# Edge layer of a two-layer graph network: four products of nil matrices ahead of each step's sums

## What is computed

```python
def _L1_gnn_ref(x, src, dst, W_w, W_b, U_w, U_b, V_w, V_b, attn_l, attn_r, gamma, beta):
    Wh = x @ W_w + W_b;  Uh = x @ U_w + U_b;  Vh = x @ V_w + V_b
    out_src = Wh * attn_l
    out_dst = Wh * attn_r
    sigma = sigmoid(out_src[src] + out_dst[dst])
    sum_sigma_h = segment_sum(Vh[src] * sigma, dst, num_segments=N)
    sum_sigma = segment_sum(sigma, dst, num_segments=N)
    h = Uh + sum_sigma_h / (sum_sigma + 1e-06)
    h = relu(layernorm(h) * gamma + beta)
    return x + h
```

## Time and profile before

| | us |
|---|---|
| median of 3 runs | 3466.37 |
| lowest, highest | 3463.25, 3470.77 |
| profiled execution | 3458.42 |
| its span, first to last instruction | 3456.7 |

### The profile page before, as it was taken

How to read it: one execution, slowest core, us unless ns; L and a number is a source line. 1 busy time by engine, 2 the same in 40 slices (tenths; PEclk the granted TensorE clock), 3 DMA queues, 4 the chain that set the end, 5 groups by cost and what they waited for, 6 DMA issues and landing times. The chain is left out here.

```text
span 3456.7 us, 52465 instructions
## 1 busy us (share of the span) xinstructions
PE 2747.0 (79%) x18168; PEld 1414.3 (41%) x18169; DVE 2561.1 (74%) x5315; ACT 1164.8 (34%) x2305; POOL 1386.3 (40%) x1623
## 2 busy tenths in 40 slices
PE   6999969999969999944886856777777777774698
PEld 3555533433443433442564411333333333333586
DVE  7999979999959999973843957677776766762354
ACT  6777740000020000021111124555555555552232
POOL 2555530000000000002046877777777777731343
PEclk9999989999979999957998966666666666766899
DMA  6000010000040000004232577888888888843411
GB/s 203 9 9 9 9 32 13 13 13 13 5 71 13 13 13 14 5 12 132 80 93 61 160 232 235 241 241 240 242 241 240 240 240 242 241 138 126 153 48 32
DMA packets 243127, 377.64 MB, mean 109 GB/s; under 512 B 83648, under 2 KB 172917, under 8 KB 241067
## 3 DMA queue, kind: packets, MB, share of 16 engines
q0 software_dynamic: 79440, 247.13, 24.1%
q1 hardware_dynamic: 148795, 112.25, 11.2%
q10 hardware_dynamic: 14624, 14.88, 1.3%
HBM read 324.13 MB, written 51.75 MB: 109 GB/s over the span
## 5 line engine op out<-in xcount | busy, mean ns | idle before, releaser
L1111 PE MATMUL dense_p_o<-dense_W,feat 128*32 128x512 f32 (+1 forms) x8400 | 879.8, 543 | 23.8 <-DVE dense_W L1053 23.7
L1053 DVE SCALAR_TENSOR_TENSOR dense_W<-layer_B,steep,cnt 128x512 f32<-128x512 f32 (+1 forms) x1400 | 848.7, 678 | 51.2 <-PE dense_p_o L1111 47.8
L2246 POOL DMA_INDIRECT strips_G<-tab_d,ixq x784 | 756.0, 964 | 243.2 <-issue 237.4
L1111 PEld LDWEIGHTS dense_p_o<-dense_W,feat 128*32 128x32 f32 x8400 | 361.6, 109 | 512.9 <-DVE dense_W L1053 226.0
L2415 PE MATMUL strips_p_sg<-strips_sv,strips_oh 128*32 128x512 f32 x2000 | 384.8, 854 | 107.4 <-DVE strips_sv L2286 107.4
L1495 POOL MEMSET route_up<- 128x128 f32 x1 | 0.2, 206 | 1006.9 <-POOLq L145 1006.9
L2403 PE MATMUL strips_p_b<-strips_wrs,strips_ohT 96*128 96x256 bf16 x1000 | 210.0, 350 | 233.6 <-DVE strips_ohT L2257 208.9
L2276 DVE TENSOR_TENSOR strips_tv<-strips_G,strips_p_b 128x1024 f32<-128x1024 f32 (+1 forms) x250 | 264.2, 1057 | 176.1 <-PE strips_p_b L2403 73.3
L2286 DVE TENSOR_TENSOR strips_sv<-strips_G,strips_p_s 128x1024 f32<-128x1024 f32 (+1 forms) x250 | 262.9, 1052 | 142.8 <-ACT strips_p_s L2360 142.3
L2360 ACT ACTIVATE strips_p_s<-strips_tv 128x1024 f32<-128x1024 f32 (+1 forms) x250 | 225.0, 900 | 301.9 <-DVE strips_sv L2286 287.8
L693 POOL TENSOR_SCALAR mix_L<-mix_back,encode_lowT 128x128 bf16<-128x128 f32 x392 | 249.9, 655 | 170.5 <-PE mix_p_c L851 170.4
(11 more groups left out here) (422 smaller groups left out, 3784.6 us busy)
## 6 DMA issues: line engine op xcount, KB each, us to landing
strips_row<-dlr_d SPq DMA_DIRECT2D x250, 96.0 KB
experts_ew<-in_ew SPq DMA_DIRECT2D x16, 1024.0 KB
strips_G<-tab_d,ixq POOLq DMA_INDIRECT x784
layer_B<-rise_d SPq DMA_DIRECT2D x12, 1024.0 KB
dense_Wd<-in_fWd ACTq DMA_DIRECT2D x1, 8192.0 KB
tab_d<-feat SPq DMA_DIRECT2D x50, 128.0 KB, 2.5
tab_d<-gated_in_rowg SPq DMA_DIRECT2D x25, 256.0 KB, 2.0
wr_d<-gated_in_wp SPq DMA_DIRECT2D x25, 192.0 KB
```

What stands on the lines that cost most here:

```text
L1053: o = nc.vector.scalar_tensor_tensor(out=out, in0=rise, scalar=C.steep[:, q * H + h:q * H + h + 1], in1=count, op0=ALU.max, op1=ALU.mult)
L1111: m = nc.tensor.matmul(p_o[c % 2][h * MT:(h + 1) * MT, a, 0:n], feat[:, q, h, lo:lo + MT], W[t % 2][:, h, 0:n], start=(q == 0), stop=(q == ...
L2246: gp.indirect_dma_start(out=G[n % RING][:, part(g) + j, :], out_offset=None, in_=C.tab3[:, :], in_offset=bass.IndirectOffsetOnAxis(ap=inde ...
```

## The change

A tile of zeros, 128 x 512 in bfloat16, is filled by VectorE at the start of the edge layer, with a semaphore of its own, on which TensorE waits once, at g = 1. In each step but a block's first, between the expansion for step g+2 and the sums of step g, TensorE multiplies the first 128 columns of that tile with the whole of it, four times, and adds the result, zeros, to the open sums. Nothing else changes: 225 of the 250 steps have four products more. In step 0 of a block there are none, since the sums are not open there yet.

```diff
-        oh = [sb(f"oh{k}", [P, H, QP]) for k in range(4)]
+        oh = [sb(f"oh{k}", [P, H, QP]) for k in range(4)]; nil = sb("nil", [P, 2 * D], BF16)
...
+                    nc.vector.memset(nil[:, :], 0.0).then_inc(s_nil, 1)
                     masks(0)
                     masks(1)
...
                     def group(g):
                         if g + 2 < NG4:
                             expand(g + 2)
+                        if g == 1:
+                            pe.wait_ge(s_nil, 1)
+                        if g % QC:
+                            for n in range(4):
+                                nc.tensor.matmul(p_sg[:, :], nil[:, 0:P], nil[:, :], start=False, stop=False)
                         sums(g)
```

More of the change, by code:

```diff
@@ L2139, in stage_strips @@
         s_gm = [sem(f"s_gm{k}") for k in range(RING)]
-        s_row = [sem(f"s_row{k}") for k in range(RR)]; s_ip = sem("s_ip"); s_wr = [sem(f"s_wr{k}") for k in range(3)]; s_oT = sem("s_oT"); s_oh = sem("s_oh"); s_b = sem("s_b"); s_t = sem("s_t")
+        s_row = [sem(f"s_row{k}") for k in range(RR)]; s_ip = sem("s_ip"); s_wr = [sem(f"s_wr{k}") for k in range(3)]; s_oT = sem("s_oT"); s_nil = sem("s_nil"); s_oh = sem("s_oh"); s_b = sem("s_b"); s_t = sem("s_t")
         s_s = sem("s_s"); s_s2 = sem("s_s2"); s_use = sem("s_use"); s_sg = sem("s_sg"); s_tot = sem("s_tot")
```

## The result

The changed kernel took 3446.11 us (median of 4 runs, 3440.16 to 3447.83), the kernel before 3467.43 (4 runs, 3463.25 to 3470.77). The ratio is 0.9936, 95% interval 0.9919 to 0.9953: 21 us faster, 0.6%. The profiled execution took 3440.16 us (span 3438.5) against 3458.42, so 18.3 us less. The forecast was 3447 and 3439.2.

A forecast was written before the change was run, and what follows sets the result against it. Consumer bounds the edge layer narrowly, gathers right behind; block 44.34 - 2.5 - 1.62 + 0.85 + 0.2 = 41.3 us. Block 24 17.8 us earlier, plus 3.1, less 1.7: net 19.2, so 3439.2 profiled, about 3447 median; range 3438 to 3470.

The forecast's parts named there:

- The two rates: Edge layer: GpSimd's gathers need 43.1 us a block, the consumer (VectorE, ScalarE, TensorE in turn) takes 44.34 in block 17.
- Memset and wait: Zero tile's fill before VectorE's first masks, and TensorE's new wait at step 1: both priced at nothing.
- The nil group's price: Four zero products in a step cost TensorE 0.85 us at the higher clock, 1.70 at the lower; weight loads hidden.
- the term of +0.85: Step 7's zero products, between expansion and second half of the hidden layer, delay VectorE's next expansion: 0.85 us a block.
- The clock: Unbroken TensorE work from step 2 raises the clock near 2746 us in block 16, instead of 2766.
- rival B: Zero products don't raise the clock, or not for long, and their time lands in the chain: 3556 us at worst; chance 0.16.
- Gain at step 4: Faster sums (0.88 us) and logits (1.63 us) ahead of ScalarE's copy and VectorE's 5.80 us wait: 2.5 us a block.
- Steps 5 to 8: Later in the block, warm sums and hidden products save 1.62 us, read from block 10's 42.72 us against 44.34.
- The bound behind it: The supplier's 43.1 us a block comes next: 1.8 of the 3.1 us gained per block only become waits for DMA.
- The distance and the end: Block 24's first gather to first sum falls to 14.5 us: 17.8 us earlier, 3.1 more within it, less 1.7; net 19.2.
- every block is like blocks up to 6: With a faster consumer, each block catches up with the gathers at step 6 and then falls behind.
- Rival A: Clock falls back at step 4 or 5, costing 2.6 us: 43.9 us a block, 3460 us in all; chance 0.16.

## Why the prediction was right, point by point

**The two rates.** Right. Gathers took 43.2 us a block (43.1 forecast), and with them taken away the kernel before gained only 0.3%: its consumer was the bound by that narrow a margin. The consumer's 44.3 us was a little high for all blocks; alone it runs at 43.7 in the mean. And "once a block" holds for block 5 only: the 23 waits for gathers of before lie in blocks 0 to 5, two each in blocks 3 and 4.

**Memset and wait.** Nothing, as forecast. The fill takes 0.27 us at 2014.07, and VectorE then still idles for 1.40 us on its row of indices, 1.88 before.

**The nil group's price.** 0.85 us at the higher clock was taken from the products of the first stage. After has it directly, in the timeline of steps 7 and 8:

```profile
2758.79 0.60 PE L2404 MATMUL strips_p_b<-strips_wrs,strips_ohT 96*128 96x256 bf16 x4
...
2763.46 0.60 PE L2404 MATMUL strips_p_b<-strips_wrs,strips_ohT 96*128 96x256 bf16 x4
```

From the one expansion to the next, with nil products, sums and half a hidden layer between, are 4.67 us. Before, the same expansions stood 3.81 us apart (2767.46 and 2771.27): 0.86 more. It reaches VectorE as the 0.87 at the opening sum above. So the term of +0.85 is right and so is its place. Weight loads cost nothing, as I chose against the Trainium skill, TensorE: Matmul & The Clock Gate, "The mechanism": each nil product has a load of its own, and in the 0.86 us of four products is no room for them beside the products. (That section also names a background weight buffer as a case in which a load is pulled ahead; that would agree with the trace.)

```profile
L2427 PEld LDWEIGHTS strips_p_sg<-strips_nil x900: 95/98/152, 2038.1 to 3106.1; 128*128 128x128 bf16 x180
L2427 PE MATMUL strips_p_sg<-strips_nil x804: 377/378/634, 2038.8 to 3106.3; 128*128 128x512 bf16 x161
```

(Columns: durations in ns, min/median/max, and first and last start. By the rule, 0.39 us a step would have come on top of the 0.85.)

**The clock.** Right in kind: products of zeros do raise it, and rival B is refuted. The Trainium skill's statement on that ("What's actually happening" on the same page: activity releases the throttled state; it says nothing of values) agrees with the 0.67 that became 0.87; that other values would do the same wasn't tried. Right in time too. The idle stretch ahead of step 2 lies behind VectorE's division and statistics of step 1; the prediction calls these the normalisation, which comes at step 3, ahead of step 4's expansion. Behind it TensorE goes like this in block 16:

```profile
2736.11 0.61 PE L2404 MATMUL strips_p_b<-strips_wrs,strips_ohT 96*128 96x256 bf16 x4 [3.81 <-DVE strips_ohT L2257]
2736.56 1.74 PE L2427 MATMUL strips_p_sg<-strips_nil 128*128 128x512 bf16 x4
2738.24 1.94 PE L2416 MATMUL strips_p_sg<-strips_sv,strips_oh 128*32 128x512 f32 x8
2740.10 0.61 PE L2404 MATMUL strips_p_b<-strips_wrs,strips_ohT 96*128 96x256 bf16 x4
...
2741.51 1.06 PE L2416 MATMUL strips_p_sg<-strips_sv,strips_oh 128*32 128x512 f32 x8
```

The first expansion still takes 0.61 us, so in this block the restart isn't cold, as the prediction has it: the clock falls just behind it. One group of nil products then takes 1.74 us and the sums 1.94; then the durations halve, 4.0 us after the restart at 2736.11. I had given 5.4 (2740.56 to 2746), where before needed some 26. No other stretch of this block is slow. The cold price of 1.70 us is right: in block 14, where the restart is cold, step 2's sums start 2.67 us behind the expansion (2646.42 to 2649.09), in before's step 6 it was 0.96 (2761.63 to 2762.59), so 1.71 more.

**Steps 4 to 8.** Gain at step 4: 2.5 forecast, 2.66 measured. Steps 5 to 8: 1.62 forecast, 1.17 at the narrow steps (0.25 - 0.36 + 1.28). The price at step 7: 0.85 against 0.87. The consumer's block: 41.3 forecast, 40.98 measured. What was mis-sized is small and went both ways. Since 41.3 was taken off a block of 44.34 us and the mean without nil products is 43.7, the gain per block is less than forecast: 3.1 forecast, 2.9 in the pair of blocks above, 2.7 in the mean.

**The bound behind it.** Right. "1.8 of the 3.1 us per block lead to nothing but waits for DMA": the waits are there, 54 of them (none in blocks 15, 16 and 18, which come in or behind the slow logits told of below), and the runs without gathers give back what they hid, 59 us in place of 21.

**The distance and the end.** The sum was right, its parts less so, and that they cancel is luck. Rows of after, the first gather and first sum of block 24 and its last product:

```profile
3050.92 0.96 POOL L2246 DMA_INDIRECT strips_G<-tab_d,ixq  x1 [0.30 <-issue]
...
3063.35 1.22 DVE L2276 TENSOR_TENSOR strips_tv<-strips_G,strips_p_b 128x1024 f32<-128x1024 f32 x1 [3.27 <-issue]
...
3101.60 0.42 DVE L2286 TENSOR_TENSOR strips_sv<-strips_G,strips_p_s 128x256 f32<-128x256 f32 x1 [1.15 <-PE strips_p_sg L2416]
```

The distance is 12.43 us, not 14.5. The step that failed is the one from step 6 to the next step 0. I took block 5's 19.11 us, which already had a wait for a gather in it, as if it compared with block 16's 20.94, which had none. While VectorE waits for a gather, TensorE goes on with the logits, so that part of the wait comes off later. In block 23 of after:

```profile
3047.04 1.22 DVE L2276 TENSOR_TENSOR strips_tv<-strips_G,strips_p_b 128x1024 f32<-128x1024 f32 x1 [1.25 <-DMA strips_G<-tab_d,ixq]
3050.52 1.22 DVE L2286 TENSOR_TENSOR strips_sv<-strips_G,strips_p_s 128x1024 f32<-128x1024 f32 x1 [1.80 <-ACT strips_p_s L2361]
```

The sum waits 1.25 us, and the product behind it 1.80 us instead of 3.13: 1.33 less. From this sum to the next opening sum are 16.31 us, where the kernel without gathers has 17.59 (my forecast: 17.9). Before's block 5 has it too: its sum waits 1.31 us and the product behind it 4.40, not 5.80.

The 12.43 us has chance in it as well. From block 5 on the distance lies between 12.0 and 17.2 us, 14.0 in the mean, and is longest behind the blocks whose logits ran slow. A block 24 close behind such blocks would have ended the stage up to 4.8 us later, which the prediction's "every block is like blocks up to 6" has no room for.

Against it, the gathers came later than "the supplier's times stay" says. Block 24's first one starts at 3050.92, before at 3047.05. Of these 3.9 us, 1.7 are a stage that began later (2013.53 against 2011.80; over the traces of all runs the first gather lies between 2011.8 and 2022.5), and 2.1 a slightly slower supply: the page has a mean of 967 ns a gather instead of 964, some 2 us over 784 of them. Gathers needed 43.14 us a block before and 43.15 with one nil product a step, 43.2 to 43.4 where the consumer keeps up with them. It looks as if a supplier without slack is slowed by those that it feeds; the cause stays open.

So block 24 starts 16.0 us earlier (17.8 forecast), runs 3.4 us shorter (3.1), and from its last product to the last logits the stage takes 33.77 instead of 32.53 us, 1.2 more (1.7 forecast for two nil groups in front of the last sums). Together 18.2 us (19.2 forecast). That the median comes within 1 us of 3447 is luck too: the medians lie 21 us apart, the profiled executions 18.3. The stage's last step is at 3135.4 us, for "near 3134".

```profile
3103.67 1.03 PE L2427 MATMUL strips_p_sg<-strips_nil 128*128 128x512 bf16 x4
...
3105.63 1.04 PE L2427 MATMUL strips_p_sg<-strips_nil 128*128 128x512 bf16 x4
```

Sums follow each of them, and both groups stand on the path, where the earlier trace rows had one row of sums.

**Rival A** happened in a part of the blocks. In blocks 14, 15 and 17 the clock is down at the logits:

```profile
2789.55 3.58 PE L2452 MATMUL strips_p_h<-strips_wg,strips_HT 128*128 128x8 f32 x16
```

These blocks take 44.1 to 45.3 us, and the clock is high at step 4's expansion and falls ahead of the logits. As the prediction said, the slack behind the gathers absorbs it: the blocks that follow catch up. Without gathers it never happened. Waits for data alone aren't the cause either, as with fewer gathers on the chip where they land late the logits took 1.95 us in nearly every block of 47.8. TensorE's idle stretch ahead of step 4's expansion goes with it: 1.4 to 1.6 us in every block without gathers, 2.74 to 3.11 in these three. But blocks 16 and 19 had 2.79 and 2.85 us and kept the clock, so its length alone doesn't settle it. What makes the clock fall in some blocks and not in others stays open.

**Not tried or open:** whether products of other values act alike; the price of one nil group alone in a measured time; the chips on which gathers land late; the 0.1 to 0.2 us that gathers lose. Nil products in six steps, the transposes first, and both together lie within the interval of the changed kernel, so none of them is shown to be better. By these rows the next gain would have to come from the gathers' 1.27 us.

## What to carry to other kernels

Fill TensorE's gaps only where a wait behind it ends last, and price two things apart: what the higher clock takes off that wait, and how far the next bound lies behind. Here 59 us of gain met a supplier that let 21 through. First look whether the slow work can simply be moved behind what the others wait for: swapping the order of two pieces gave the same time as 900 added products. And when comparing stretches of two blocks, see whether a wait lies in one of them; the other engines go on working in it.

## What the runs showed of the hardware

- Four nil products in nine of ten steps raised the granted clock of the layer from 0.67 to 0.87 and made every kind of product shorter in the mean (the logits, 8 columns wide, 3.58 to 1.95 us in most blocks). One product in each of these steps raised the mean to 0.74 and left the logits at 3.58 us: the clock rose in step 3 and was mostly down again behind 3.2 to 3.5 us of idle time. Only these two doses were run.
- With all data at hand and nil products in place, a granted clock that had risen stayed up through a stretch of 16 logits products between two waits, in every block (0.89 in the mean).
- Nearly the same program (nil products at step 7 alone, against the changed kernel) had 186 GB/s in the layer on one chip and 232 on another, at the same 957 ns of issue a gather, and the kernel before took 3467 or 3795 us. A gain measured on one kind need not be there on the other: nil products gained 59 us where data was at hand; with fewer gathers where data came late, they took 5 us more on one chip, within the noise, and gained 15 on another.
